# Attention on one core: a new issue order for five engines, and output stores moved from SyncE to ScalarE

## The reference

```python
q, k, v = jnp.split(x @ W_qkv.T + b_qkv, 3, axis=-1)      # 16 heads, 32 columns each
scores = jnp.einsum('bqhe,bkhe->bhqk', q, k) * scale
scores = jnp.where(causal, scores, -jnp.inf)
attn = jax.nn.softmax(scores, axis=-1)
out = jnp.einsum('bhqk,bkhe->bqhe', attn, v)
```

## Time and profile before

| what | value |
|---|---|
| median of 3 runs | 1739.25 us (1739.24 to 1741.14) |
| the profiled execution | 1735.57 us |
| its span, first to last instruction | 1733.7 us |
| mean granted TensorE clock | 0.985 of full speed |
| PE, PEld busy | 1661.0 us (96%), 1295.1 us (75%) |
| DVE, ACT, POOL busy | 1018.7, 655.5, 557.8 us |

### The profile page before, as it was taken

How to read it: one execution, slowest core, us unless ns; L and a number is a source line. 1 busy time by engine, 2 the same in 40 slices (tenths; PEclk the granted TensorE clock), 3 DMA queues, 4 the chain that set the end, 5 groups by cost and what they waited for, 6 DMA issues and landing times. The chain is left out here.

```text
span 1733.7 us, 21900 instructions
## 1 busy us (share of the span) xinstructions
PE 1661.0 (96%) x7804; PEld 1295.1 (75%) x7804; DVE 1018.7 (59%) x1667; ACT 655.5 (38%) x1271; POOL 557.8 (32%) x540
## 2 busy tenths in 40 slices
PE   5999999999999999999989989989999999999998
PEld 3676888788788877876656656658888888888887
DVE  4321365564623454358988989855655555555785
ACT  4421322232213332228878878762222222222221
POOL 4201210310310003117777767672144031033320
PEclk9999999999999999989999999999999999999999
DMA  7200210110101038843554545323010010012243
GB/s 287 102 12 1 61 49 19 55 31 20 60 7 37 25 108 250 291 170 75 121 120 106 122 112 133 79 73 129 0 52 25 1 49 25 1 49 71 76 133 134
DMA packets 101916, 141.80 MB, mean 82 GB/s; under 512 B 43881, under 2 KB 52713, under 8 KB 100274
## 3 DMA queue, kind: packets, MB, share of 16 engines
q1 hardware_dynamic: 100946, 134.05, 26.4%
q10 hardware_dynamic: 864, 6.39, 1.2%
HBM read 93.74 MB, written 46.53 MB: 81 GB/s over the span
## 5 line engine op out<-in xcount | busy, mean ns | idle before, releaser
L1538 ACT ACTIVATE prob<-p_turn 128x512 f32<-128x512 f32 (+3 forms) x384 | 176.2, 487 | 56.9 <-PE p_turn L1510 36.9
L1577 DVE TENSOR_TENSOR pt_lo<-prob,pt_hi 128x512 fp32r<-128x512 f32 (+3 forms) x256 | 173.7, 703 | 33.7 <-ACT pt_hi L1546 33.2
L1570 DVE TENSOR_REDUCE row_top<-p_score 128x1 fp32r<-128x128 f32 (+7 forms) x256 | 184.6, 746 | 14.4 <-PE p_score L1494 12.5
L1025 DVE TENSOR_TENSOR hid<-hid,p_up 128x512 f32<-128x512 f32 x64 | 44.0, 687 | 218.2 <-PE p_up L490 202.5
L1593 POOL TENSOR_TENSOR pt_lo<-prob,pt_hi 128x512 fp32r<-128x512 f32 (+1 forms) x128 | 167.0, 1305 | 10.7
L1924 DVE TENSOR_TENSOR e_hid<-e_hid,e_p_up 128x512 f32<-128x512 f32 x64 | 44.0, 687 | 196.4 <-PE e_p_up L1819 196.4
L1524 PE MATMUL p_o<-pt_hi,v 128*65 128x512 f32 (+3 forms) x384 | 137.9, 362 | 3.9 <-POOL pt_lo L1593 2.3
L1590 POOL TENSOR_SCALAR pt_hi<-prob 128x512 fp32r<-128x512 f32 (+1 forms) x128 | 100.9, 788 | 106.3 <-ACT prob L1538 64.2
L1525 PE MATMUL p_o<-pt_lo,v 128*65 128x512 f32 (+3 forms) x384 | 128.5, 341 | 0.0
L1546 ACT ACTIVATE pt_hi<-prob 128x512 fp32r<-128x512 f32 (+3 forms) x256 | 120.6, 486 | 3.2 <-PE p_o L1525 0.2
L772 ACT ACTIVATE hid<-p_gate 128x512 f32<-128x512 f32 x64 | 38.3, 599 | 218.7 <-PE p_gate L490 218.6
(11 more groups left out here) (279 smaller groups left out, 4256.7 us busy)
## 6 DMA issues: line engine op xcount, KB each, us to landing
stack<-qk_parked SPq DMA_DIRECT2D x66, 256.0 KB, 4.9
raw<-in_wgu SPq DMA_DIRECT2D x64, 256.0 KB, 2.7
qk_parked<-qk SPq DMA_DIRECT2D x16, 1024.0 KB, 4.0
v_parked<-v_out SPq DMA_DIRECT2D x16, 520.0 KB, 7.4
o_parked<-o_both SPq DMA_DIRECT2D x64, 128.0 KB
stack_third<-qk_parked SPq DMA_DIRECT2D x30, 256.0 KB, 4.4
v<-v_parked ACTq DMA_DIRECT2D x6, 1040.0 KB, 8.3
res<-in_x SPq DMA_DIRECT2D x8, 512.0 KB
```

Of the source, the lines that this page charges most:

```text
L1538: act.activation(prob[:, n % PB, c0:W], p_turn[:, n % TB, c0:W], ACT.Exp).then_inc(exped, 1)
L1570: dve.tensor_reduce(top[:, h % 2, r:r + 1], p_score[:, r % 2, 0:width_of(r)], AX_X, ALU.max, negate=True).then_inc(topped, 1)
L1577: dve.tensor_tensor(pt_lo[:, n % PT, c0:W], prob[:, n % PB, c0:W], pt_hi[:, n % PT, c0:W].bitcast(F32), ALU.subtract).then_inc(split, 1)
```

## The change

The five lists of `ORDER` are replaced, `store` goes from SP's list, and its two DMAs are issued by ACT inside `read_o`, behind a wait for the copy just issued. The instructions are otherwise the same ones, in the same number; buffers and semaphores are unchanged.

```diff
     ORDER = {
-        "tensor": [("weigh", 0, 0), ("weigh", 1, 0), ("score", 5, 1), ("weigh", 2, 0), ("weigh", 3, 0), ("turned", 6, 0),
-                   ("score", 6, 1), ("turned", 7, 0), ("turned", 8, 0), ("weigh", 4, 0), ("weigh", 5, 0), ("score", 7, 1),
-                   ("score", 0, 2), ("turned", 9, 0), ("turned", 10, 0), ("turned", 11, 0), ("weigh", 6, 0),
-                   ("weigh", 7, 0), ("turned", 0, 1), ("score", 1, 2), ("score", 2, 2), ("turned", 1, 1),
-                   ("turned", 2, 1), ("weigh", 8, 0), ("weigh", 9, 0), ("score", 3, 2), ("weigh", 10, 0),
-                   ("weigh", 11, 0), ("score", 4, 2), ("turned", 3, 1), ("turned", 4, 1), ("turned", 5, 1)],
-        "scalar": [("exp", 3, 0), ("exp", 4, 0), ("round", 3, 0), ("exp", 5, 0), ("round", 5, 0), ("read_o", 0, 0),
-                   ("exp", 6, 0), ("exp", 7, 0), ("exp", 8, 0), ("round", 7, 0), ("exp", 9, 0), ("exp", 10, 0),
-                   ("round", 9, 0), ("exp", 11, 0), ("round", 10, 0), ("round", 11, 0), ("exp", 0, 1),
-                   ("round", 0, 1), ("exp", 1, 1), ("exp", 2, 1), ("round", 2, 1), ("read_o", 1, 0)],
-        "vector": [("top", 4, 1), ("rest", 2, 0), ("rest", 3, 0), ("top", 5, 1), ("rest", 5, 0), ("top", 6, 1),
-                   ("rest", 7, 0), ("top", 7, 1), ("top", 0, 2), ("rest", 9, 0), ("top", 1, 2), ("top", 2, 2),
-                   ("rest", 10, 0), ("rest", 11, 0), ("rest", 0, 1), ("top", 3, 2)],
+        "tensor": [("score", 0, 2), ("turned", 6, 0), ("weigh", 0, 0), ("weigh", 1, 0), ("weigh", 2, 0), ("weigh", 3, 0),
+                   ("turned", 7, 0), ("turned", 8, 0), ("score", 1, 2), ("score", 2, 2), ("weigh", 4, 0), ("turned", 9, 0),
+                   ("weigh", 5, 0), ("score", 3, 2), ("turned", 10, 0), ("score", 4, 2), ("weigh", 6, 0),
+                   ("turned", 11, 0), ("score", 5, 2), ("weigh", 7, 0), ("turned", 0, 1), ("turned", 1, 1),
+                   ("weigh", 8, 0), ("turned", 2, 1), ("turned", 3, 1), ("score", 6, 2), ("weigh", 9, 0),
+                   ("weigh", 10, 0), ("weigh", 11, 0), ("turned", 4, 1), ("turned", 5, 1), ("score", 7, 2)],
+        "scalar": [("exp", 5, 0), ("exp", 6, 0), ("round", 5, 0), ("read_o", 0, 0), ("exp", 7, 0), ("exp", 8, 0),
+                   ("round", 7, 0), ("exp", 9, 0), ("round", 9, 0), ("exp", 10, 0), ("round", 10, 0), ("exp", 11, 0),
+                   ("round", 11, 0), ("exp", 0, 1), ("exp", 1, 1), ("round", 0, 1), ("exp", 2, 1), ("exp", 3, 1),
+                   ("round", 2, 1), ("round", 3, 1), ("read_o", 1, 0), ("exp", 4, 1)],
+        "vector": [("rest", 2, 0), ("rest", 3, 0), ("top", 7, 1), ("top", 0, 2), ("rest", 5, 0), ("top", 1, 2),
+                   ("top", 2, 2), ("top", 3, 2), ("rest", 7, 0), ("top", 4, 2), ("top", 5, 2), ("rest", 9, 0),
+                   ("rest", 10, 0), ("rest", 11, 0), ("top", 6, 2), ("rest", 0, 1)],
         "gpsimd": [("divide", 4, 0), ("divide", 6, 0), ("divide", 8, 0), ("divide", 1, 1)],
-        "sync": [("place", 4, 1), ("store", 0, 0), ("place", 5, 1), ("place", 6, 1), ("place", 7, 1),
-                 ("stack", 2, 0), ("place", 0, 2), ("place", 1, 2), ("place", 2, 2), ("place", 3, 2), ("store", 1, 0)],
+        "sync": [("place", 7, 1), ("place", 0, 2), ("stack", 2, 0), ("place", 1, 2), ("place", 2, 2),
+                 ("place", 3, 2), ("place", 4, 2), ("place", 5, 2), ("place", 6, 2)],
     }
...
-            def store(h, g):
-                b, pr, a = place_of(h)
-                sp.wait_ge(o_read, G * h + g + 1)
-                row, t0, i = E * (2 * pr + a), b * S + g * W, (G * h + g) % OS
-                sp.dma_start(o_dram[h // HB, :, row:row + E, t0:t0 + W], o_both[0:2 * E, i]).then_inc(o_stored[i], 16)
-                sp.dma_start(sum_dram[TT * (h // HB) + G * b + g, row // E:row // E + 1], o_both[2 * E:VC, i])\
-                    .then_inc(o_stored[i], 16)
...
                 act.activation(o_both[:, i], p_o[0:VC, :], ACT.Copy).then_inc(o_read, 1)
+                b, pr, a = place_of(h)
+                row, t0 = E * (2 * pr + a), b * S + g * W
+                act.wait_ge(o_read, G * h + g + 1)
+                act.dma_start(o_dram[h // HB, :, row:row + E, t0:t0 + W], o_both[0:2 * E, i]).then_inc(o_stored[i], 16)
+                act.dma_start(sum_dram[TT * (h // HB) + G * b + g, row // E:row // E + 1], o_both[2 * E:VC, i])\
+                    .then_inc(o_stored[i], 16)
```

More of the change, by code:

```diff
@@ L1465, in place @@
                              top[:, h % 2, r:r + 1].bitcast(F32)).then_inc(placed[r // QB], 16)
-            def store(h, g):
-                b, pr, a = place_of(h)
-                sp.wait_ge(o_read, G * h + g + 1)
-                row, t0, i = E * (2 * pr + a), b * S + g * W, (G * h + g) % OS
-                sp.dma_start(o_dram[h // HB, :, row:row + E, t0:t0 + W], o_both[0:2 * E, i]).then_inc(o_stored[i], 16)
-                sp.dma_start(sum_dram[TT * (h // HB) + G * b + g, row // E:row // E + 1], o_both[2 * E:VC, i])\
-                    .then_inc(o_stored[i], 16)
             sp.wait_ge(*qk_last)
-            run({"stack": next_stack, "place": place, "store": store}, ORDER["sync"])
+            run({"stack": next_stack, "place": place}, ORDER["sync"])
         @block.tensor
```

## The result

| | before | after |
|---|---|---|
| median of the runs timed together | 1740.2 us (1739.24 to 1741.59) | **1766.95 us** (1765.11 to 1768.55) |
| ratio of after to before, 95% interval | | **1.0153** [1.0135, 1.0170] |
| span of the profiled execution | 1733.7 us | 1766.1 us |
| mean granted TensorE clock | 0.985 | 0.978 |

The change costs 26.7 us, 1.5%. The forecast was 1737 us, in a range of 1718 to 1751: the time lies above it.

A forecast was written before the change was run, and what follows sets the result against it. No engine was busy throughout before; after the change ACT was to bound the attention at 11.57 us a head. 31 x (11.57 - 11.74) = -5.3, +3 at the start, gave -2.3 on 1739.25: 1737 us, range 1718 to 1751.

The forecast's parts named there:

- Rows further ahead: PE's scoring of rows 7 and 3: placing waits go, 11.74 us a head falls towards 10.96, at most 0.8 a head.
- a landing of 8.5 us at most: Row-maxima placings: rows scored over 10 us before the block that needs them, against this longest landing, so placing waits go.
- rival C: ACT's issues cheap or hidden: round 10.9 us, 1716 us in all; half way 11.2 and 1726; chance 0.21.
- What would be late next is half of a q and k stack ... I cost it at nothing: Stack load on SP: wanted about a head after issue; 0 us counted, uncovered a few us in one round of two.
- Stores come to ACT: ACT's in-order queue: 1.69 us per copy with its store against 0.49, making ACT's round 11.47 us and the bound.
- The long issues that I added 0.1 for: ACT's round: 0.1 us a head for issues longer than the median and short waits, giving 11.57.
- Order of subtractions: DVE's 512-wide subtractions colliding with POOL: at best 0.38 us saved on each colliding one, counted as nothing.
- Start: First attention round, three more rows scored before the first exponentials catch up: +3 us, bounds 1 and 4.
- A: The forecast: ACT-bound at 11.45 to 11.75 us a head, 1733 to 1743 us; chance 0.46.
- B: ACT loses time at its copies (L1555) waiting for `p_o`: 11.93 us a head, 1748 us, up to 1760; chance 0.27.
- the 4 and the 8 that I had set as signs: Total waits of ACT's copies (L1555) for `p_o`: under 4 us expected, over 8 means B.
- D: Issues of SP's and ACT's queues exclude each other: some 0.5 us a head, 1752 us; chance 0.06.

The follow-up runs named there:

- the small stores: The whole change, but ACT's result store moves 16 of 512 columns, 4 KB instead of 128 KB, with all issues kept: 1734.83 us, 0.9967 of the kernel before.
- the sum stored by SP: The whole change, but the sums are stored by SP again, so ACT issues one DMA per copy: 1756.59 us, 1.0109 of the kernel before.
- the order alone: The kernel before with the new order lists, stores left on SP: 1726.39 us, 0.9921 of the kernel before.
- split values: The whole change with each value load split into four parts of 260 KB over four heads, and `load_next` moved: 1742.55 us, 1.0011 of the kernel before.
- the stores alone, old order: The kernel before with its old order, both stores of each copy moved from SP to ACT: 1805.93 us, 1.0379 of the kernel before.
- the sum stored alone: The kernel before with its old order, ACT storing only the sum and SP the result: 1759.13 us, 1.0109 of the kernel before.

## Why the prediction was wrong

*Rows further ahead: right in part, and worth more than I said.* The waits for `row_top` fell, and with the stores on SP an undisturbed head takes 10.2 to 10.5 us. I had let nothing fall under 10.96, but for rival C's 10.9. What didn't hold is the cover, "a landing of 8.5 us at most": with ACT storing, two placings beside each value load take 9.3 us or more, and one beside the last takes 15.7. PE has room for most of that (its longest wait is 4.5 us); SP, which waits for them in order, has not.

*"What would be late next is half of a q and k stack ... I cost it at nothing": the step that failed.* I named the transfer, its place and the size of the wait, "a few us in one round of two", and then let it be free. It is issued behind the first two placings of a round and wanted at the start of the next, "as before": that part held, 8.1 to 8.5 us before, and 8.2 to 8.7 in the changed kernel where it isn't late (the small stores). But I never read how long it took to land, about 7 us, so I didn't see that the margin was some 1.3 us. And I moved the stores' issues from queue to queue in the sum, but not their 8.4 MB. On SP's queue they stand behind the stack; on ACT's one is issued 0.5 us after the stack and travels beside it. That makes the landing 8.5 to 10.3 us and the margin nothing. The second thing that I didn't read is SP's wait for its own placings: behind a value load it puts off the stack's issue by some 2.3 us, for which there was no margin left. Measured, the term is 21.1 us of waits for q and k, 19.1 of them in six rounds, and the slower clock behind them. With the small stores 32 us of the time go away, without the value loads 28.

*Stores come to ACT: right to 0.03 us.* 11.47 worked out, 11.50 measured, with issues of 0.493 and 0.480 us (I had 0.53 and 0.45). The long issues that I added 0.1 for are not there: one issue of 128 takes 1.28 us, all others under 0.7. With the small stores the head has 11.5, and 11.9 behind a value load. The fit to 0.03 is partly luck, since two errors of 0.03 to 0.04 in the issues cancel, and the sum stored by SP leaves it open whether a cheaper ACT would have shortened every head.

*Order of subtractions: nothing, as counted, and the collisions are not gone.* VectorE's 512-wide subtractions in the changed kernel:

```profile
L1575 DVE TENSOR_TENSOR pt_lo<-prob,pt_hi 128x512 fp32r<-128x512 f32 x96 | 83.4, 869 | 45.2 <-ACT pt_hi L1538 42.8
```

869 ns against 878 before: the new order takes collisions from the narrow ones (384 wide 601 against 993 ns, 128 wide 424 against 568), and hardly from the 512-wide that I looked at.

*Start: +4.0 us, the upper bound of what I gave it.* From the first score to the first copy it is 16.1 us before and 20.1 after, 19.2 with the order alone: 3.1 us for the order and 1.0 for the stores. The other 1.6 of the 5.6 us are a later beginning of the phase (first score at 770.86 against 769.28), which lies between 768.0 and 773.0 in the traces of this case and has nothing to do with the change.

*The sum.* Undisturbed 31 x (11.50 - 11.74) = -7.4 us; late transfers and slow stretches 31 x (12.61 - 11.50) = **+34.4 us**; start +5.6, tail -0.4. The second term had 3 us in my sum, the 0.1 us a head for long issues and short waits, and none of it for a late transfer. How it parts between the waits and the lower clock behind them I can't tell: no run has one without the other.

*The rivals.* A's mechanism is there underneath: 1734.83 with small stores, 1742.55 with split values, both inside A's band of 1733 to 1743. B, which gave the right sign, was wrong in its reason: copies wait 6.3 us in all, between the 4 and the 8 that I had set as signs, and 2.3 with the small stores. C falls with issues of 0.49 and 0.48. D falls too, by a row in which ScalarE issues both its DMAs while SP issues stacks; the first row below is ScalarE's queue, the last SP's.

```profile
838.52 0.50 ACTq L1551 DMA_DIRECT2D o_parked<-o_both  x1
839.05 0.51 ACTq L1552 DMA_DIRECT2D sum_parked<-o_both  x1
```

```profile
837.93 2.06 SPq L1153 DMA_DIRECT2D stack<-qk_parked  x3
```

Of the 64 large stores 48 overlap an issue of SP and 16 don't; the median of either kind is 0.493 us. SP's run shown takes 2.06 us where the one at 851.77 takes 1.53, but over all its stack issues the median is 0.43 us with an issue of ACT beside it and without. The Trainium skill (Perfetto Trace Analysis, section "DMA Instruction — HWDGE (DVE, Sync)") has the generator locked by one issue at a time; by its medians this trace doesn't agree with a lock between these two queues. It also says in that section that the profiled issue doesn't contain the movement of the data, and there the trace agrees, 0.43 us for an issue against 4.9 to land: the term that I left out is just what such an issue doesn't show.

The range was too narrow because each of its cases priced instructions. None had a late transfer in it, though the text said that one was next.

## What to carry to other kernels

When a DMA's issue moves to another queue, its bytes move too: write down for each transfer that somebody waits for when it is issued, when it lands, when it is wanted, and what travels beside it and ahead of it. A margin of about 1 us on a landing of 7 is no cover at nothing; price it as a wait, and price what the clock does behind it. Look at what the issuing engine itself waits for: a small DMA whose landing it awaits in order puts off the next large issue by as much as it is late. If a large transfer makes others late, moving it only changed the victim here, and issuing the victim earlier made the ones behind it late; splitting it gave the whole change 24 us, and the order alone no more than its interval.

## What the runs showed of the hardware that I had not expected

- **A small DMA behind large ones can take as long as they do**: with both halves of a stack issued early, 0.5 KB behind six transfers of 256 KB took 15 us (958.42 to 973.2), against 4.2 for a placing in the median. Yet the three placings issued next took 9.2 to 9.8 us and landed ahead of the sixth transfer. The Trainium skill (DMA: Bandwidth & Descriptors, section "Queues, rings and completion order") has a transfer's semaphore written only after every earlier write of that DMA engine; the 15 us agree with it, and which DMA engines a placing ran on the trace doesn't tell.
- **A store issued on ACT's queue together with a stack on SP's delays the stack**: with the same issues, stores of 128 KB beside a stack make three transfers of 256 KB land after 8.5 to 10.3 us, stores of 4 KB after 6.4 to 7.9. Where ACT issues the 128 KB 4.0 us behind the stack (the stores alone, old order) it is 6.1 to 8.2, so the other queue by itself isn't enough. The Trainium skill (DMA: Bandwidth & Descriptors, section "Issuing engines are not separate DMA queues") says that queues of different engines run on the same 16 DMA engines, so that a second one saves only time to issue; that landings on SP's queue move with the bytes on ACT's agrees. It would have been the rule to weigh ahead of the forecast. But the 16 engines are busy for only 0.50 of the landing from 925.18 to 934.34, against 0.58 for one of the kernel before (941.54 to 948.98), so their throughput isn't used up; what stretches the landing isn't shown.
- **The sum's issue costs 0.22 us by itself and 0.48 right behind another one** on the same queue (ScalarE's rows above, of the kernel after and of the sum stored alone), so about half of the 0.48 looks like waiting for the issue ahead.
- **What a hold of an in-order engine costs hangs on the order around it**: 2.40 us of holds a head gave 2.94 us more in the old order and some 1.1 in the new one. Why is not shown.
